# A two-layer transformer with expert routing on one core: GpSimd's scatters and gathers without their waits for TensorE's signals, and ten scatters, not sixteen, in the attention block

## The chip, the core and the metric

The kernel runs on 1 core of one Trainium2 chip. Its engines are TensorE (PE in the profile, PEld for its weight loads), VectorE (DVE), ScalarE (ACT), GpSimd (POOL) and SyncE (SP), which issues transfers. The metric is the device time of one execution in microseconds; a version's time is the median of its runs.

## What is computed

Two layers over 1024 tokens of 256 features, each with attention and a mixture of experts, and a layer norm ahead of each of the four parts:

```
x = x + L0_attn(layernorm(x))      # 16 heads, softmax attention over a triangular solve
x = x + L0_ffn(layernorm(x))       # 64 experts of width 96, top 8, at most 256 tokens each
x = x + L1_attn(layernorm(x))      # linear attention: elu features, cumulative sums
x = x + L1_ffn(layernorm(x))       # 8 experts of width 512, top 2
```

What the change touches is the routing of `L0_ffn`. Each token's normed row goes to its eight experts, and the eight results come back weighted:

```
xbuf = zeros((E, C, D)).at[e_sorted, pos].set(x[tok_sorted], mode='drop')
y = einsum('ecf,edf->ecd', silu(g) * u, w_down)     # g, u: projections of xbuf
out = zeros((N, D)).at[tok_sorted].add(y[e_sorted, safe_pos] * (s_sorted * valid)[:, None])
```

## The kernel before

The kernel has three blocks, one after the other; at the end of a block every engine drains and they meet in a barrier. Their ends are lines L341, L1342 and L1694 in the profile.

**Attention block** (to L341): the first layer's attention. The tokens are in two halves of four tiles of 128 rows (`HT` = 4, `NT` = 8). The first half is done earlier than the second: its rows are normed, its expert choice is made, and GpSimd begins to scatter it into `expert_rows` in DRAM, while the rest of the attention is still being done. `scatter(pool, k, t, rows)` (L199) sends the 128 rows of tile t to the slot of each row's k-th expert. A half has 32 scatters (k = 0 to 7, t = 0 to 3), and the first `EARLY` of the first half stand in this block.

**Expert block** (to L1342): the second half's norm, its choice of experts, the other scatters of the first half (L1527 to L1533), the 32 of the second (L1535 to L1546), and then the 64 experts. A token's eight slots are in the order of their experts, so the k-th slot of a token belongs to expert k or a later one. Therefore SyncE loads the rows of expert e (`load_rows`, L1572) for e below 8 when the scatters of k = e of all eight tiles have landed (`s_gb[e]` at 128). Weights come two experts at a time (`load_weights`); SyncE issues the fourth group behind `load_rows` of expert 7. Per expert TensorE turns the rows (`s_t`), does gate and up (`s_gu`), turns the hidden values (`s_th0`) and projects down (`s_y0`); two experts are in flight. At the end GpSimd gathers the results of k = 0 and 1 (16 gathers, L1558), as soon as the experts that these can name are stored.

**Last block** (to L1694): GpSimd gathers k = 2 to 7 (48 gathers, L2116; gather g uses buffer g % 16 and may start when addition g - 16 is done, `s_acc0`). VectorE adds each gathered tile to `X` (`add_gathered`, L1939). The tokens are in four quarters of twelve gathers (`GQ`), and each quarter goes through the linear attention while the next is added up: norm (`norm_lin`), TensorE turns (`s_tr`) and projects (`s_pr`), ScalarE makes the features (relu and exp, L1874 to L1880), VectorE makes products and running sums (`window`, L1950 to L1957), and TensorE projects out (`s_oo`). VectorE's order is written out:

```
for q in range(1, NQ):
    gathered(q, 0, 3)
    if q > 1:
        add_outputs(q - 2)
        norm_ffn(q - 2)
    add_bias(q - 1)
    gathered(q, 3, 8)
    window(q - 1, 0)
    gathered(q, 8, 11)
    window(q - 1, 1)
    gathered(q, 11, GQ)
    norm_lin(q)
```

Behind it come the second choice of experts, 16 scatters, and 23 tiles of the second mixture of experts.

Many of GpSimd's transfers have a wait for a semaphore that TensorE raises and whose work they don't read: these are the waits of the change. Beside them stand waits that the data need: `s_idx` (slots ready), `s_zf` (rows zeroed), `s_st` (results stored), `s_acc0` (buffer free).

## Time and profile before

| | before |
|---|---|
| median of 3 runs | 1025.71 us (1023.77 to 1027.04) |
| profiled execution, its own time | 1016.34 us |
| its span, first to last instruction | 1014.6 us |
| mean granted TensorE clock | 0.837 of full |
| busy: TensorE / VectorE / ScalarE / GpSimd | 70% / 54% / 31% / 25% |
| indirect transfers by GpSimd | 64 scatters, 16 + 48 gathers, 16 scatters, 23 additions to the output |

All times in rows are microseconds from the start of the span of the one profiled execution, if not marked ns. A busy share is a mean over blocks that have different limits. A name with q (POOLq, DVEq) is the engine's sequencer, which waits, drains and branches; it runs ahead of the engine. GpSimd's busy time for an indirect transfer is the time to issue it, and the transfer lands later. What a row names as the releaser of a wait is inferred.

### The profile page before, as it was taken

Reading aid. Unit: us, or ns where it says so; the run is one execution under the profiler, and the core shown is the slowest. Engines: PE = TensorE matmul, PEld = TensorE weight load, DVE = VectorE, ACT = ScalarE, POOL = GpSimd, SP = SyncE. Lnnn points to the kernel's source line nnn. Section 1 sums busy time; section 2 is a strip of 40 time slices with the busy share of each in tenths; the row PEclk is TensorE's granted clock in tenths of the full one; section 3 lists DMA queues with packets and bytes.
Section 4 is the critical chain, followed back from the end, with each engine's and each line's share of the span. In section 5 each row is a group of like instructions: output and inputs, shape, how many; then the busy total and the mean of one; then the engine's idle time right before and its main releaser. Section 6 shows DMA issues by size and latency. Waiting matters only on the chain. (4 is left out here: it accounts for less than half of the span.)

```text
span 1014.6 us, 17699 instructions
## 1 busy us (share of the span) xinstructions
PE 708.1 (70%) x6542; PEld 566.9 (56%) x6587; DVE 549.2 (54%) x1652; ACT 313.5 (31%) x535; POOL 252.2 (25%) x258
## 2 busy tenths in 40 slices
PE   4858377858757786973156999999205763599995
PEld 2423265446436545842145999999204542599994
DVE  6896986799499679263501333333146675022221
ACT  1004143542444355432022444444003451111110
POOL 6003011120211111016762000000575626023222
PEclk9988779979887898597577999999756675699998
DMA  4981002340631358204947888887422204688760
GB/s 136 137 130 48 0 2 46 156 63 3 199 51 14 125 211 319 96 17 146 320 142 251 288 290 291 294 283 248 130 76 68 81 26 156 244 229 249 221 195 1
DMA packets 75561, 151.73 MB, mean 150 GB/s; under 512 B 12768, under 2 KB 36064, under 8 KB 72544
## 3 DMA queue, kind: packets, MB, share of 16 engines
q1 hardware_dynamic: 62064, 124.27, 39.7%
q0 software_dynamic: 10224, 21.12, 7.4%
q10 hardware_dynamic: 3200, 5.38, 1.6%
q8 instruction: 44, 0.72, 0.3%
q14 instruction: 29, 0.24, 0.1%
HBM read 91.01 MB, written 60.43 MB: 149 GB/s over the span
## 5 line engine op out<-in xcount | busy, mean ns | idle before, releaser
L1375 PE MATMUL scores<-wgu,zero 128*128 128x192 f32 x512 | 98.2, 337 | 3.7 <-DMA wd<-in_wd 3.7
L750 DVE TENSOR_REDUCE block_maxima<-scores 128x10 f32<-128x1280 f32 x64 | 92.3, 1486 | 7.7 <-PE scores L400 6.7
L1032 ACT ACTIVATE E<-scores 128x1280 f32<-128x1280 f32 x64 | 77.3, 1238 | 60.6 <-PE scores L411 32.4
L1476 DVE TENSOR_TENSOR gated_up<-gated,scores 128x192 f32<-128x192 f32 x64 | 22.7, 354 | 123.7 <-ACT gated L1517 123.7
L1375 PEld LDWEIGHTS scores<-wgu,zero 128*128 128x128 f32 x512 | 85.6, 197 | 3.9 <-DMA wd<-in_wd 3.9
L1815 PE MATMUL scores<-xgT,w 128*128 128x128 f32 x736 | 87.8, 278 | 0.0
L1815 PEld LDWEIGHTS scores<-xgT,w 128*128 128x128 f32 x736 | 86.0, 196 | 0.1
L1170 POOL TENSOR_SCALAR_AFFINE_SELECT E<-E 128x256 f32<-128x256 f32 x64 | 27.2, 449 | 205.8 <-ACT E L1032 205.7
L1508 ACT COPY zero<-misc 128x512 f32<-128x512 f32 x64 | 37.5, 586 | 98.3 <-PE misc L1368 98.3
L1392 PE MATMUL scores<-wd,gated_turned 96*128 96x256 f32 x256 | 67.0, 385 | 0.5 <-ACT gated_turned L1504 0.5
L2116 POOL DMA_INDIRECT gb<-expert_outputs,gather_slots x48 | 55.0, 1147 | 33.7 <-DVE X L1939 17.0
L1368 PE MATMUL misc<-cf,xg 128*128 128x128 f32 x256 | 40.3, 281 | 32.7 <-DMA xg<-expert_rows 32.7
L2141 POOL DMA_INDIRECT out<-yb,add_to x23 | 35.5, 1544 | 111.0 <-DVE yb L2079 109.0
L1558 POOL DMA_INDIRECT gb<-expert_outputs,gather_slots x16 | 16.4, 1024 | 171.5 <-DMA expert_outputs<-xnT 164.9
L1468 DVE COPY xnT<-scores 128x512 f32<-128x512 f32 x64 | 44.3, 692 | 25.6 <-PE scores L1392 25.6
L2092 DVE TENSOR_TENSOR cum<-low,scores 128x512 f32<-128x512 f32 x23 | 15.8, 689 | 77.2 <-issue 67.8
L1368 PEld LDWEIGHTS misc<-cf,xg 128*128 128x128 f32 x256 | 32.4, 144 | 41.5 <-issue 19.5
L400 PE MATMUL scores<-cb 128*128 128x128 bf16 x256 | 53.5, 230 | 1.8 <-issue 0.7
L825 DVE TENSOR_TENSOR tmp<-Y,LB 128x120 f32<-128x120 f32 (+35 forms) x244 | 49.7, 242 | 0.3
L834 DVE TENSOR_TENSOR Y<-Y,tmp 128x120 f32<-128x120 f32 (+35 forms) x244 | 49.6, 242 | 0.1
L199 POOL DMA_INDIRECT expert_rows<-stack_q,scatter_slots x32 | 31.5, 984 | 66.4 <-issue 61.3
L1392 PEld LDWEIGHTS scores<-wd,gated_turned 96*128 96x128 f32 x256 | 44.5, 194 | 4.4 <-ACT gated_turned L1504 0.7
(295 smaller groups left out, 1500.4 us busy)
## 6 DMA issues: line engine op xcount, KB each, us to landing
w<-in_w SPq DMA_DIRECT2D x23, 1024.0 KB, 5.0
expert_rows<-zero SPq DMA_DIRECT2D x32, 512.0 KB, 6.2
xg<-expert_rows SPq DMA_DIRECT2D x64, 256.0 KB, 3.2
expert_outputs<-xnT SPq DMA_DIRECT2D x64, 256.0 KB, 3.0
wgu<-in_wgu SPq DMA_DIRECT2D x32, 384.0 KB, 3.6
rows_by_expert<-zero SPq DMA_DIRECT2D x21, 408.0 KB, 6.0
wd<-in_wd SPq DMA_DIRECT2D x32, 192.0 KB, 3.8
w<-in_w ACTq DMA_DIRECT2D x8, 512.0 KB, 10.3
```

What stands on the lines that cost most here:

```text
L400: ins = nc.tensor.matmul(scores[:, slot, o + w - P:o + w], identb, mask[c, it], start=False, stop=True)
L750: nc.vector.tensor_reduce(bm[:, c, h, :], scores[:, slot, 0:WIDE].rearrange("p (a n) -> p a n", n=P), AX.X, ALU.max).then_inc(s_fd, 1)
L825: nc.vector.tensor_tensor(part, Yc[:, x, 0:n, k:k + 1].to_broadcast([P, n, w]), LB[:, k:k + 1, k + 1:SB].to_broadcast([P, n, w]), ALU.mult ...
L834: nc.vector.tensor_tensor(below, below, part, ALU.add).then_inc(s_inv, 1)
L1032: nc.scalar.activation(to[:, h, :], scores[:, k % 2, 0:WIDE], ACT.Exp, scale=SCALE).then_inc(s_fa, 1)
L1368: ins = nc.tensor.transpose(misc[:, j % 2, c:c + P], xg[:, j, t, k * P:(k + 1) * P], identf)
L1375: ins = nc.tensor.matmul(scores[:, j % 2, t * 2 * F0:(t + 1) * 2 * F0], xgT[:, j % 2, k, t * P:(t + 1) * P], wgu[:, j // GE, j % GE, k, :] ...
L1392: ins = nc.tensor.matmul(scores[:, j % 2, 1024 + t * D:1024 + (t + 1) * D], hT[:, j % 2, t * P:(t + 1) * P], wd[:, j // GE, j % GE, :], st ...
L1468: nc.vector.tensor_copy(yb[:, j % NY].rearrange("p t d -> p (t d)"), scores[:, j % 2, 1024:1536]).then_inc(s_yv, 1)
L1508: nc.scalar.copy(xgT[:, j % 2].rearrange("p k n -> p (k n)"), misc[:, j % 2, :]).then_inc(s_xt0, 1)
L1815: ins = nc.tensor.matmul(scores[:, j, c:c + P], w13[:, q, k, c:c + P], xgT[:, j, k, :], start=(k == 0), stop=(k == KT - 1))
L2116: pool.indirect_dma_start(out=gb[:, g % NG, :], out_offset=None, in_=ybuf, in_offset=bass.IndirectOffsetOnAxis(ap=ig[:, t, k:k + 1], axis= ...
```

## The change

The waits for `s_us`, `s_o`, `s_ot`, `s_tr`, `s_lg`, `s_rk`, `s_y0`, `s_t`, `s_th0`, `s_gu`, `s_oo` and `s_pr` ahead of GpSimd's scatters and gathers are taken out, and `EARLY` is 10 in place of 16. No other engine's program changes.

```diff
-EARLY = 16
+EARLY = 10
...
                     for g in range(EARLY):
-                        if g == 4:
-                            pool.wait_ge(s_us, 4 * UNITS)
-                        if g == 6:
-                            pool.wait_ge(s_o, 2 * UNITS - 1)
-                        if g == 8:
-                            pool.wait_ge(s_o, 2 * UNITS)
-                        if g == 9:
-                            pool.wait_ge(s_ot, 2 * UNITS)
-                        if g == 11:
-                            pool.wait_ge(s_tr, 10)
                         scatter(pool, g // HT, g % HT, xn0[:, g % HT, :])
...
                     for g in range(EARLY, HT * K0):
-                        if g == EARLY + 4:
-                            pool.wait_ge(s_tr, 12)
-                        if g == EARLY + 8:
-                            pool.wait_ge(s_lg, 2)
-                        if g == EARLY + 12:
-                            pool.wait_ge(s_rk, 2)
                         scatter(pool, g // HT, g % HT, xn0[:, g % HT, :])
                     pool.wait_ge(s_idx, 4)
                     for k in range(K0):
                         for t in range(HT):
-                            if t == 0 and k > 5:
-                                pool.wait_ge(s_y0, k - 5)
-                            if t == 1 and k > 1:
-                                pool.wait_ge(s_t, k - 1)
-                            if t == 2 and k > 4:
-                                pool.wait_ge(s_th0, k - 4)
-                            if t == 3 and k > 2:
-                                pool.wait_ge(s_gu, k - 2)
                             scatter(pool, k, HT + t, xn[:, t, :])
...
                         if g == NT:
                             pool.wait_ge(s_st[1], 16 * ((E0 - K0) // NY + 1))
-                        if g % 2:
-                            pool.wait_ge(s_gu, min(E0, E0 - 2 + g // 2))
-                        elif g:
-                            pool.wait_ge(s_y0, min(E0, E0 - 5 + g // 2))
...
                     for g in range(NG, NT * K0):
                         t, k = gather_at(g)
-                        q, r = divmod(g - NG, GQ)
                         pool.wait_ge(s_acc0, g - NG + 1)
-                        if r == 3 and q > 1:
-                            pool.wait_ge(s_oo, QT * (q - 1))
-                        if r == 4 and q:
-                            pool.wait_ge(s_tr, 12 + at_lin(q - 1) + 1)
-                        if r == 7 and q:
-                            pool.wait_ge(s_pr, 2 * q - 1)
-                        if r == 8 and q > 1:
-                            pool.wait_ge(s_tr, 12 + at_ffn(q - 2) + 1)
-                        if r == 10 and q:
-                            pool.wait_ge(s_pr, 2 * q)
```

GpSimd's program at the end of the attention block, as a difference (each row is one or more scatters; in brackets the semaphores waited for, by their names, `attended` being `s_o` and `transposed` being `s_tr`):

```order
-L199 DMA expert_rows<-stack_q,scatter_slots 16384x256 x3
-L199 DMA expert_rows<-stack_q,scatter_slots 16384x256 [waits solve_u]
-L199 DMA expert_rows<-stack_q,scatter_slots 16384x256
-L199 DMA expert_rows<-stack_q,scatter_slots 16384x256 [waits attended]
-L199 DMA expert_rows<-stack_q,scatter_slots 16384x256
-L199 DMA expert_rows<-stack_q,scatter_slots 16384x256 [waits attended]
-L199 DMA expert_rows<-stack_q,scatter_slots 16384x256 [waits o_turned]
-L199 DMA expert_rows<-stack_q,scatter_slots 16384x256
-L199 DMA expert_rows<-stack_q,scatter_slots 16384x256 [waits transposed]
-L199 DMA expert_rows<-stack_q,scatter_slots 16384x256 x4
+L199 DMA expert_rows<-stack_q,scatter_slots 16384x256 x9
 L341 UNCONDITIONAL_BRANCH
```

Ahead of these rows stands one more scatter in both. Six scatters have moved behind the block's end.

GpSimd's program at the start of the expert block, before, from the block's first scatter (`stack_q` holds the first half's rows, `xn_moe` the second's):

```order
L199 DMA expert_rows<-stack_q,scatter_slots 16384x256 x4
L199 DMA expert_rows<-stack_q,scatter_slots 16384x256 [waits transposed]
L199 DMA expert_rows<-stack_q,scatter_slots 16384x256 x3
L199 DMA expert_rows<-stack_q,scatter_slots 16384x256 [waits logits]
L199 DMA expert_rows<-stack_q,scatter_slots 16384x256 x3
L199 DMA expert_rows<-stack_q,scatter_slots 16384x256 [waits ranks]
L199 DMA expert_rows<-stack_q,scatter_slots 16384x256 x3
L199 DMA expert_rows<-xn_moe,scatter_slots 16384x256 [waits slots_ready]
L199 DMA expert_rows<-xn_moe,scatter_slots 16384x256 x8
L199 DMA expert_rows<-xn_moe,scatter_slots 16384x256 [waits rows_turned]
```

and the same stretch of the changed kernel, up to the gathers at the block's end:

```order
L1515 UNCONDITIONAL_BRANCH [waits barrier_Pool_Activation_PE_DVE_SP_gather]
L199 DMA expert_rows<-stack_q,scatter_slots 16384x256 x22
L199 DMA expert_rows<-xn_moe,scatter_slots 16384x256 [waits slots_ready]
L199 DMA expert_rows<-xn_moe,scatter_slots 16384x256 x31
L1530 DMA gb<-expert_outputs,gather_slots 128x256 [waits y_stored2,y_stored3,y_stored1,y_stored0]
```

The 16 scatters of the first half that stood here are 22, and the only wait left among the 54 is the one for the slots.

GpSimd's gathers in the last block, before, from the first of quarter 1 that has such a wait (the 16 ahead of it wait for `row_added` alone; `lin_projected` is `s_pr`, `lin_out` is `s_oo`):

```order
L2116 DMA gb<-expert_outputs,gather_slots 128x256 [waits transposed,row_added]
L2116 DMA gb<-expert_outputs,gather_slots 128x256 [waits row_added] x2
L2116 DMA gb<-expert_outputs,gather_slots 128x256 [waits lin_projected,row_added]
L2116 DMA gb<-expert_outputs,gather_slots 128x256 [waits row_added] x2
L2116 DMA gb<-expert_outputs,gather_slots 128x256 [waits lin_projected,row_added]
L2116 DMA gb<-expert_outputs,gather_slots 128x256 [waits row_added] x4
L2116 DMA gb<-expert_outputs,gather_slots 128x256 [waits lin_out,row_added]
```

In the changed kernel all 48 are one row that waits for `row_added`.

## Rows read from the trace of the kernel before

**Rows 1.** Windows: length, busy us (instructions) by engine, granted clock, DMA share, GB/s.
```profile
600.00:700.00 100.00, 100.00 (x639) 93.27 (x638) 36.83 (x71) 41.60 (x106) 0.00 (x0) 1.00 0.85 291
```

**Rows 2.** Timeline of GpSimd's scatters: start, length; in brackets idle time before, releaser.
```profile
451.40 1.18 POOL L199 DMA_INDIRECT expert_rows<-stack_q,scatter_slots  x1 [52.88 <-issue]
...
470.78 0.97 POOL L199 DMA_INDIRECT expert_rows<-stack_q,scatter_slots  x1 [0.31 <-issue]
474.86 0.97 POOL L199 DMA_INDIRECT expert_rows<-stack_q,scatter_slots  x1 [3.12 <-POOLq L341]
...
481.02 0.97 POOL L199 DMA_INDIRECT expert_rows<-stack_q,scatter_slots  x1 [1.34 <-PE misc L163]
...
512.19 0.97 POOL L199 DMA_INDIRECT expert_rows<-xn_moe,scatter_slots  x1 [4.30 <-issue]
...
540.29 0.97 POOL L199 DMA_INDIRECT expert_rows<-xn_moe,scatter_slots  x1 [0.30 <-issue]
```

**Rows 3.** Timeline of TensorE in the first experts.
```profile
510.00 1.09 PE L1368 MATMUL misc<-cf,xg 128*128 128x128 f32 x4 [19.37 <-DMA xg<-expert_rows]
...
549.75 2.61 PE L1375 MATMUL scores<-wgu,zero 128*128 128x192 f32 x7 [3.66 <-DMA wd<-in_wd]
```

**Rows 4.** The block ends' lines: drains, ns min/median/max, first and last start.
```profile
L341 POOLq DRAIN  x1: 11013/11013/11013, 462.9 to 462.9; - x1
L341 DVEq DRAIN  x1: 17/17/17, 465.4 to 465.4; - x1
...
L1342 POOLq DRAIN  x1: 13496/13496/13496, 720.9 to 720.9; - x1
```

**Rows 5.** Timeline of GpSimd's gathers at the expert block's end.
```profile
709.42 1.03 POOL L1558 DMA_INDIRECT gb<-expert_outputs,gather_slots  x1 [2.24 <-PE scores L1375]
...
728.12 1.02 POOL L1558 DMA_INDIRECT gb<-expert_outputs,gather_slots  x1 [0.30 <-issue]
```

**Rows 6.** GpSimd's waits from 760 to 820: total, times, longest.
```profile
POOL gb L2116 <- DVE X L1939: 9.6, 6, 3.8
...
POOL gb L2116 <- PE misc L1730: 2.9, 1, 2.9
```

**Rows 7.** Timeline of GpSimd's gathers in the last block.
```profile
737.86 4.84 POOL L2116 DMA_INDIRECT gb<-expert_outputs,gather_slots  x1 [0.30 <-DVE X L1939]
743.01 1.02 POOL L2116 DMA_INDIRECT gb<-expert_outputs,gather_slots  x1 [0.30 <-issue]
...
784.27 1.02 POOL L2116 DMA_INDIRECT gb<-expert_outputs,gather_slots  x1 [3.00 <-DVE X L1939]
```

**Rows 8.** Line 2107, GpSimd's wait for `s_oo`: ns min/median/max, first and last start.
```profile
L2107 POOLq EVENT_SEMAPHORE  x2: 17/17/17, 783.5 to 804.3; - x2
```

**Rows 9.** Timeline of VectorE: both windows of quarters 0, 1 and 2 begin.
```profile
773.32 0.68 DVE L1950 TENSOR_TENSOR relu<-relu,low 128x512 f32<-128x512 f32 x1
...
775.62 0.87 DVE L1939 SCALAR_TENSOR_TENSOR X<-gb,w,X 128x256 f32<-128x256 f32 x2
...
777.19 0.68 DVE L1950 TENSOR_TENSOR relu<-relu,low 128x512 f32<-128x512 f32 x1
...
794.01 0.69 DVE L1950 TENSOR_TENSOR relu<-relu,low 128x512 f32<-128x512 f32 x1
...
797.92 0.68 DVE L1950 TENSOR_TENSOR relu<-relu,low 128x512 f32<-128x512 f32 x1
...
814.60 0.68 DVE L1950 TENSOR_TENSOR relu<-relu,low 128x512 f32<-128x512 f32 x1
...
818.60 0.69 DVE L1950 TENSOR_TENSOR relu<-relu,low 128x512 f32<-128x512 f32 x1
```

**Rows 10.** Timeline of ScalarE: the last relu of the first window's features, quarters 0 to 2.
```profile
770.58 0.82 ACT L1880 ACTIVATE relu<-scores,bias_lin 128x256 f32<-128x256 f32 x2
...
792.74 0.82 ACT L1880 ACTIVATE relu<-scores,bias_lin 128x256 f32<-128x256 f32 x2
...
813.38 0.82 ACT L1880 ACTIVATE relu<-scores,bias_lin 128x256 f32<-128x256 f32 x2
```

## The prediction

> **What bounds the kernel now.** I read the windows view first, to see which engine has no idle time in which stretch, then GpSimd's own timeline, and then, for each of its pauses, what stands behind it. In the middle of the expert stage TensorE is busy 100.00 of 100.00 us at full granted clock [rows 1], so nothing that GpSimd does there counts. Before it, however, GpSimd is the pacer: from 451.40 to 541.27 us it issues 64 scatters, each 0.97 us long and 1.28 us after the last one [rows 2] (from 512.19 to 540.29 there are 22 steps, 28.10 us, 1.277 us each). SyncE may load expert e's rows only when all eight scatters of k = e have landed, and it issues the fourth weight group behind the load for k = 7. TensorE starts its full run at 549.75 after a wait for exactly that group's `wd` [rows 3]. So whatever ends the last scatter earlier starts the full TensorE run earlier.
>
> The chain of scatters has three pauses beside its usual gap of 0.30 us [rows 2]: 3.12 us at 474.86 (the end of the block), 1.34 us at 481.02 (a released wait for TensorE's transposes) and 4.30 us at 512.19. The last one is put down to "issue", but it stands before the tenth scatter of the second half, which is t = 1, k = 2, and waits for `s_t` at 1. TensorE's first turned rows start at 510.00 and take 1.09 us [rows 3]: the release at 511.09 lies 1.1 us before the scatter.
>
> **The block ends.** GpSimd is last there, too. In the attention block its 16th scatter ends at 471.75, its drain at 462.9 + 11.01 = 473.9, and VectorE had reached its own drain at 465.4 [rows 4]. In the expert block the 16th gather ends at 729.14 [rows 5] and the drain at 720.9 + 13.50 = 734.4 [rows 4]. The drain outlives the last transfer's issue by 2.14 us there and by 5.3 us here. With 16 indirect transfers since the last drain at the first, 64 at the second, the tail grows by about 3.14 / 48 = 0.065 us for each, if it is their number that counts; that it is the number is my reading of two points.
>
> **The change, term by term.** The sum is made against the profiled execution (1016.34 us, span 1014.6). The three runs lie at 1023.77 to 1027.04, 9.4 us above it at the median. I carry the difference over to the median, since nothing shown tells where those 9.4 us lie.
>
> 1. EARLY from 16 to 10. Six scatters leave the attention block: its tenth ends at 471.75 - 6 x 1.28 = 464.1 and its drain, with a tail of 2.14 (or 1.75 by the count), at 466.2 (465.8). Both are later than VectorE's 465.4, so GpSimd still ends the block, 7.7 us earlier. It restarts 0.97 us behind its drain as before (473.9, 474.86), at 467.2. The six scatters are not saved, they come behind the restart: 22 of them, 28.1 us. The second half then starts at 467.2 + 28.1 = 495.3, plus 0.1 for a few that last longer. Before, it started at 540.29 - 31 x 1.277 - 4.0 (the pause of term 2) = 496.7. So 1.3 us are won, the removed wait at 481.02 (1.34 - 0.30 = 1.04) among them. The slots of the second half come from VectorE; it starts this block 7.7 us earlier, so they come no later than the scatters want them.
> 2. The waits on `s_t`, `s_gu`, `s_th0`, `s_y0` between the second half's scatters. Only the pause at 512.19 has a price: 4.30 - 0.30 = 4.0 us. The others stood at 0.30 us and cost nothing. GpSimd's last scatter ends 5.3 us earlier, and with it come the load for k = 7, the weights behind it and TensorE's full run: **-5.3 us**.
> 3. The waits between the 16 gathers at the end of the expert block. The second gather waited 2.24 us for TensorE [rows 5], 1.9 above the usual gap. These gathers end the block, so all of it counts: **-1.9 us**. The drain's tail has six scatters more behind it, +0.4 us by the count and nothing otherwise; the first block's tail is shorter by the same. I take 0 for the two together.
> 4. The waits between the 48 gathers of the last block. GpSimd is idle there 9.6 us in six pauses put down to VectorE's additions, and 2.9 us in one put down to TensorE [rows 6]. The name in the first is misleading: the gather at 784.27 [rows 7] is number 43 and needs only the 28 additions ahead of `norm_lin(0)`, a quarter and more back; the sequencer's own wait on `s_oo` (L2107) stands at 783.5, 0.8 us ahead of it [rows 8]. These pauses go too. But the gathers run 16 buffers ahead and VectorE has a second supplier, the projections by TensorE and ScalarE that feed `window`. What is won is only the time from "features ready" to "window started". VectorE starts the first window of quarters 0 to 2 at 773.32, 794.01 and 814.60 [rows 9]; ScalarE's last `relu` ends at 771.40, 793.56 and 814.20 [rows 10]. With some 0.05 us of signalling that is 1.87, 0.40 and 0.35 us. Between the two windows stand three additions at 0.40 us, and the first window takes 2.30 us (773.32 to 775.62), so 3.50 us from window to window where there were 3.87, 3.91 and 4.00 [rows 9]: 0.37, 0.41 and 0.50 us. Sum: **-3.9 us**. Everything behind `norm_lin(3)` is ordered by VectorE, TensorE and the slots, with no removed wait in it.
>
> The moved instructions cost nothing else: no transfer is added, SyncE's and ScalarE's queues keep their order, and only start 7.7 us sooner. Sum: 5.3 + 1.9 + 3.9 = 11.1 us. 1016.34 - 11.1 = 1005.2 for a profiled execution, 1025.71 - 11.1 = **1014.6 us** for the median.
>
> **Bounds.** If the last block took over all of GpSimd's 12.5 us in those seven pauses less seven usual gaps (2.1), it would win 10.4 in place of 3.9, in all 17.6: 1008.1. If it won nothing, 7.2 in all: 1018.5. For the drains, an end below: both tails at the shorter 2.14 would give 3.2 more.
>
> **Rivals.**
> - *Only the expert stage pays.* The quarters stay as long as they are, because some step of TensorE's and ScalarE's chain that I read as ready is held by another. Rows 9 and 10 speak against it, since each window starts 0.4 us or more behind the `relu` that it reads. 1018.5 us. Chance 17%.
> - *The pauses are the profile's.* The runs are 9.4 us longer than the profiled execution, so their waits may fall otherwise, and TensorE may be late by more or GpSimd by less. Then the gain is lost in what TensorE does: within 3 us of 1025.7. Chance 9%.
> - *The freed gathers hold up VectorE* (slower). While VectorE did 16 additions in a row, a gather lasted 4.84 us in place of 1.02 [rows 7]: the two share something. So far it is the gather that pays. Released from their waits, gathers start whenever they can, also ahead of VectorE's own instructions. In quarters 1 to 3 VectorE has some 30 instructions on the chain with two SBUF operands (18 in the windows, 12 additions). If each waited for half a gather, 0.51 us, that is 15.3 us, and the kernel ends 4.2 us slower, at 1029.9. It decides from 11.1 / 30 = 0.37 us each. Against it: gathers already run beside the windows, and from 772 to 820 VectorE's additions there last the same 0.4 to 0.5 us as without them. Chance 7%, with all other losses. By the Trainium skill, page "SBUF — State Buffer", section "Who interferes with whom", a VectorE instruction with two SBUF inputs contends with a GpSimd instruction that reads SBUF, and issue order decides who blocks. By that rule this rival is the outcome when gathers come first; the trace agrees with it only for gathers that come second.
> - *More than the sum.* The last block gives back up to 10.4 us, or a denser TensorE keeps a higher granted clock in the quarters. Down to 1008.1 us. Chance 9%.
> - *The forecast*, 58%, with a range of its own of 1011 to 1018.
>
> **The numbers.** A change under 0.3% (3.1 us) can't be told from none. Faster by more: 58 + 17 + 9 = 84%; within: 9%; slower: 7%. The range leaves out the no-gain and slower cases above and a little of the fastest below: 1008 to 1021.5 us, which also takes in the spread of the runs (3.3 us).
>
> **What the changed profile would show.** GpSimd's drain in the attention block ends near 466; its scatters then run from about 467 to 536 with no gap over 0.5 us; TensorE's full run starts at about 544.5. In the gathers at the expert block's end no pause is left, and the expert block's drain ends near 727.2. There, additions r = 3 to 7 of a quarter come in a row, followed by idle time that ends with ScalarE's `relu` and not with a landing. I would be wrong if the scatters get a new pause (for VectorE's slots at 495, say), if the drains grow, or if VectorE's instructions lengthen beside the gathers.

## The result: slower by 2.7%, and the profile after

| | before | after |
|---|---|---|
| median | 1024.91 us (4 runs, 1023.77 to 1027.04) | 1052.61 us (4 runs, 1051.89 to 1053.72) |
| ratio | | 1.0269, 95% interval 1.0248 to 1.0289 |
| profiled execution, its span | 1016.34, 1014.6 us | 1053.72, 1052.0 us |
| mean granted clock | 0.837 | 0.826 |

The forecast was 1014.6 us. The time is 38 us above it and lies outside the range.

GpSimd's own pauses went as forecast. This is its timeline after, every row of the scatters whose gap is not the usual 0.30 or 0.31 us, and the last of the attention block and of all. It answers to [rows 2].

```profile
453.20 1.17 POOL L199 DMA_INDIRECT expert_rows<-stack_q,scatter_slots  x1 [52.43 <-issue]
...
464.90 0.97 POOL L199 DMA_INDIRECT expert_rows<-stack_q,scatter_slots  x1 [0.31 <-issue]
480.53 0.97 POOL L199 DMA_INDIRECT expert_rows<-stack_q,scatter_slots  x1 [14.66 <-POOLq L341]
...
516.70 0.97 POOL L199 DMA_INDIRECT expert_rows<-xn_moe,scatter_slots  x1 [8.42 <-DVE gather_slots L1442]
...
556.23 0.97 POOL L199 DMA_INDIRECT expert_rows<-xn_moe,scatter_slots  x1 [0.30 <-issue]
```

Behind the first step of 1.48 us the ten scatters run 1.28 us apart, and the 32 of the second half take 39.5 us from first to last where they took 43.6. But two new gaps stand between them: 14.66 us at the block's end, 8.42 us for VectorE's slots. The last scatter starts at 556.23, 15.9 us later than before.

GpSimd no longer ends the attention block. Its drain is over at 457.8 + 9.96 = 467.8, VectorE's begins at 479.6. These rows, sequencers' drains at the block end, answer to [rows 4]; the last one is the expert block's, which ends at 754.5.

```profile
L341 POOLq DRAIN  x1: 9956/9956/9956, 457.8 to 457.8; - x1
L341 ACTq DRAIN  x1: 614/614/614, 472.3 to 472.3; - x1
L341 DVEq DRAIN  x1: 17/17/17, 479.6 to 479.6; - x1
```
```profile
L1332 POOLq DRAIN  x1: 18762/18762/18762, 735.7 to 735.7; - x1
```

Why VectorE is 14 us later shows in ScalarE's timeline of that stretch. It copies two results of TensorE (L551) into the tiles `bankT` and `bankD`, called the two banks here. Before:

```profile
454.71 0.59 ACT L1074 COPY bankT<-misc 128x512 f32<-128x512 f32 x1 [6.42 <-PE misc L551]
456.92 0.59 ACT L1074 COPY bankD<-misc 128x512 f32<-128x512 f32 x1 [1.63 <-PE misc L551]
```

After, ScalarE and then VectorE:

```profile
460.41 0.58 ACT L1074 COPY bankT<-misc 128x512 f32<-128x512 f32 x1 [10.34 <-remote]
467.68 0.59 ACT L1074 COPY bankD<-misc 128x512 f32<-128x512 f32 x1 [6.68 <-remote]
```
```profile
467.74 0.26 DVE L893 RECIPROCAL rec<-scores 128x16 f32<-128x16 f32 x1 [11.51 <-remote]
```

```
matmul ends   semaphore changes   late by   semaphore
454.81        460.39               5.58     s_o, first bank
461.02        467.66               6.64     s_o, second bank
462.52        467.71               5.20     s_ot
497.91        511.78              13.87     s_rk
793.93        803.76               9.83     s_pr
810.66        819.22               8.57     s_oo
```

By the profile TensorE's matmul is done (its end is a modelled time), the semaphore that says so changes 5 to 14 us later in these six cases, and whoever reads it sits idle. The view of waits puts 129.7 us to "remote" in 17 waits of the changed kernel, and none in the first profile of before. All 17 are waits for a semaphore that TensorE raises. Not every signal is late: of the 89 that fall while GpSimd issues scatters or gathers one behind the other, 37 have no recorded change within 0.25 us of their matmul's end, and of the other 616 one. The longest groups of "remote" (total, times, longest):

```profile
ACT gated L1507 <- remote: 22.3, 2, 18.4
DVE slot L1431 <- remote: 15.6, 1, 15.6
ACT xnT L1834 <- remote: 12.5, 1, 12.5
DVE rec L893 <- remote: 11.5, 1, 11.5
ACT bankT L1074 <- remote: 10.3, 1, 10.3
ACT low L1846 <- remote: 9.9, 1, 9.9
```

The late signals are not all of the 14.2 us. The second bank is copied 10.8 us later (467.68 for 456.92): 6.6 us of it is the late signal, and 4.2 us is that its matmuls themselves end later. These are the 64 matmuls of both banks, before and after:

```profile
450.65 6.20 PE L551 MATMUL misc<-E,xnT 128*32 128x512 f32 x64 [1.07 <-DVE xnT L881]
```
```profile
452.45 6.08 PE L551 MATMUL misc<-E,xnT 128*32 128x512 f32 x57 [1.08 <-DVE xnT L881]
458.96 0.44 PE L551 MATMUL misc<-E,xnT 128*32 128x128 f32 x5 [0.43 <-issue]
460.39 0.63 PE L551 MATMUL misc<-E,xnT 128*32 128x128 f32 x2 [0.99 <-issue]
```

The second bank's 32 took 2.2 us before and 6.2 us after, with gaps for which the profile shows no cause ("issue") and at a granted clock of 1.00 from 453 to 459. The last 3.4 us come behind the copy. While the second bank's last matmuls came with those gaps, TensorE's granted clock fell to its lower level: it was 0.50 (1.2 GHz) from 461 to 477, where it was 1.00 (2.4 GHz) from 456 to 466 before. Its three groups behind the copy took 9.0 us in place of 5.6 (1.11, 1.97 and 5.95 us for 0.66, 1.09 and 3.81).

GpSimd's gathers and the last block's first scatter (to [rows 5] and [rows 7]):

```profile
727.72 1.06 POOL L1530 DMA_INDIRECT gb<-expert_outputs,gather_slots  x1 [170.52 <-DMA expert_outputs<-xnT]
...
747.63 1.02 POOL L1530 DMA_INDIRECT gb<-expert_outputs,gather_slots  x1 [0.30 <-issue]
757.97 1.28 POOL L2077 DMA_INDIRECT gb<-expert_outputs,gather_slots  x1 [9.32 <-DVE X L1911]
759.56 4.84 POOL L2077 DMA_INDIRECT gb<-expert_outputs,gather_slots  x1 [0.30 <-DVE X L1911]
...
874.01 1.07 POOL L2093 DMA_INDIRECT rows_by_expert<-rows_ffn,slots  x1 [39.94 <-DVE slots L1960]
```

The 16 gathers have no pause left and take 19.9 us from first to last, 2.1 less than before (706.12 to 728.12). They start 21.6 us later. The gather of 4.84 us stands where it stood.

The wait of `slot` for the ranks (`s_rk`) is what delayed the second half's slots and left the gap of 8.42 us. In the last block the pauses of [rows 6] are gone, and the windows come later all the same. These are VectorE's two windows of quarter 0 and the first of quarter 1, which answer to the first three in [rows 9] (773.32, 777.19, 794.01), and ScalarE's `low` that the second of them needed:

```profile
794.02 0.69 DVE L1922 TENSOR_TENSOR relu<-relu,low 128x512 f32<-128x512 f32 x1 [2.80 <-ACT relu L1852]
806.11 0.69 DVE L1922 TENSOR_TENSOR relu<-relu,low 128x512 f32<-128x512 f32 x1 [8.51 <-ACT relu L1852]
833.19 0.69 DVE L1922 TENSOR_TENSOR relu<-relu,low 128x512 f32<-128x512 f32 x1 [5.94 <-ACT relu L1852]
```
```profile
803.78 0.84 ACT L1846 ACTIVATE low<-scores,minus_bias 128x256 f32<-128x256 f32 x2 [9.86 <-remote]
```

From the first window to the second it is 12.1 us where it was 3.87, and to the third 39.2 us where it was 20.7. VectorE's own instructions are no longer than they were, 0.69 us for this one.

### The profile page after: what moved, and what is told of

It is laid out like the page before. It is cut to its first block and busy times, and to the rows that moved or that the text cites. A ratio compares the mean times of both kernels' runs of the same rounds, so it can differ in the third digit from the quotient of the medians.

```text
span 1052.0 us, 17685 instructions
## 1 busy us (share of the span) xinstructions
PE 711.8 (68%) x6542; PEld 568.2 (54%) x6587; DVE 548.2 (52%) x1652; ACT 313.0 (30%) x535; POOL 250.7 (24%) x258
## 5 line engine op out<-in xcount | busy, mean ns | idle before, releaser
L1032 ACT ACTIVATE E<-scores 128x1280 f32<-128x1280 f32 x64 | 77.4, 1237 | 60.7 <-PE scores L411 32.4
L1382 PE MATMUL scores<-wd,gated_turned 96*128 96x256 f32 x256 | 69.1, 393 | 10.9 <-ACT gated_turned L1494 6.3
L2102 POOL DMA_INDIRECT out<-yb,add_to x23 | 35.5, 1543 | 111.2 <-DVE yb L2051 88.1
```

The costliest lines, as they stand in the source:

```text
L1032: nc.scalar.activation(to[:, h, :], scores[:, k % 2, 0:WIDE], ACT.Exp, scale=SCALE).then_inc(s_fa, 1)
L1382: ins = nc.tensor.matmul(scores[:, j % 2, 1024 + t * D:1024 + (t + 1) * D], hT[:, j % 2, t * P:(t + 1) * P], wd[:, j // GE, j % GE, :], st ...
```

## The experiments

All kernels are set against runs of the kernel before on the same chip. That matters: the experiments fell on five chips, and on one of them, here called the fifth, the kernel before took 1014.5 us where it took 1024 to 1027 on the other four. On which chips the result and the first profile of before were taken is not known. The table shows the landmarks of each profile from GpSimd's timeline: the second half's first scatter (h2), the last scatter (end), the first of the 16 gathers (g0), the first of the 48 (g16), the first scatter of the last block (r0), and the span. "Late" is how many of 705 TensorE signals have no recorded change within 0.25 us of their matmul's end. Some records of changes are missing, so this counts too many; the idle time put to "remote" is the safer column.

| kernel | its time | before beside it | late | "remote" us | h2 | end | g0 | g16 | r0 | span |
|---|---|---|---|---|---|---|---|---|---|---|
| before, first profile | 1016.34 | | 0 | 0 | 496.7 | 540.3 | 706.1 | 736.3 | 840.3 | 1014.6 |
| before, profiled again | 1025.4 | 1026.2 | 27 | 48.9 | 502.6 | 547.8 | 713.1 | 744.1 | 845.0 | 1023.7 |
| EARLY 10 alone | 1031.3 | 1024.8 | 31 | 53.9 | 507.7 | 552.8 | 717.6 | 748.1 | 851.3 | 1029.6 |
| attention block's waits out | 1035.7 | 1024.8 | 31 | 37.8 | 511.0 | 556.5 | 720.6 | 751.6 | 855.7 | 1034.0 |
| expert block's waits out | 1031.6 | 1024.8 | 28 | 66.0 | 507.1 | 546.6 | 719.4 | 750.5 | 851.8 | 1030.5 |
| last block's waits out | 1038.8 | 1024.8 | 32 | 81.2 | 501.7 | 547.2 | 713.0 | 743.6 | 859.5 | 1037.4 |
| after | 1052.6 | 1024.9 | 38 | 129.7 | 516.7 | 556.2 | 727.7 | 758.0 | 874.0 | 1052.0 |
| second half's waits out | 1027.0 | 1025.3 | 34 | 60.7 | 501.0 | 540.5 | 713.2 | 743.6 | 847.7 | 1026.1 |
| second half's waits out, on the fifth chip | 1010.5 | 1014.5 | 0 | 0 | 496.8 | 536.4 | 702.9 | 733.4 | 834.2 | 1008.7 |
| end gathers' waits out, on the fifth chip | 1014.0 | 1014.5 | 0 | 0 | 498.6 | 542.5 | 708.0 | 736.1 | 838.5 | 1012.7 |

Theory 1 was that TensorE's signals are handed on late while GpSimd issues indirect transfers without standing still for them. Theory 2 was that what is late is only a consequence: of six more scatters behind the block's end, or of VectorE's instructions held up by GpSimd's.

### The change in four parts

**EARLY 10 alone.** `-EARLY = 16`, `+EARLY = 10`, all waits kept (that at g = 11 goes with its scatter).

> The change split: here only EARLY goes from 16 to 10, and all waits for TensorE stay where they were (the one at g = 11 falls away with its scatter; those counted from EARLY move to scatters 14, 18 and 22). Theory 1 (TensorE's signals are handed on late while GpSimd issues indirect transfers one behind the other with no wait for TensorE between them) gives no loss here: no ScalarE or VectorE wait at 455 to 468, the second block starts 5 to 8 us earlier than before's 474.1 and the whole is 0 to 3 us faster than before, about 1024. Theory 2 (six more scatters behind the block's end are what pushes the experts back) gives the last scatter at 545 or later and a kernel of 1030 or more.

1031.31 us, ratio 1.0066 (1.0035 to 1.0098): slower by itself. Theory 1's numbers were wrong, and theory 2's were met (last scatter at 552.8, over 1030 us): six more scatters behind the block's end do cost time. They do because the block's end does not come sooner by as much, and its rows show why. GpSimd is through early, but VectorE reaches its drain only at 475.3 and not at 465.4 [rows 4], since its inputs are late in this profile too:

```profile
466.52 1.00 POOL L199 DMA_INDIRECT expert_rows<-stack_q,scatter_slots  x1 [0.82 <-PE scores L561]
476.24 0.97 POOL L199 DMA_INDIRECT expert_rows<-stack_q,scatter_slots  x1 [8.72 <-POOLq L341]
```
```profile
L341 POOLq DRAIN  x1: 3128/3128/3128, 466.3 to 466.3; - x1
L341 DVEq DRAIN  x1: 17/17/17, 475.3 to 475.3; - x1
```

The block ends at 475.4 where it ends at 478.1 in the second profile of before, and GpSimd starts again at 476.24 and not at 478.89: 2.6 us won for six scatters (7.7 us) that come behind it. The difference of 5.1 us is that of h2 (507.7 to 502.6).

**The attention block's waits alone.** The five `wait_ge` on `s_us`, `s_o`, `s_ot` and `s_tr` ahead of these scatters are out, EARLY is 16.

> Only the five waits for TensorE in the attention block are taken out, EARLY stays 16. Theory 1: the 16 scatters run from about 451 to 472, and what TensorE signals from 454 on reaches ScalarE and VectorE late; with six scatters more than in the changed kernel the delay is at least its 5.7 us at the block's start, so the second block starts at 480 to 487 and the kernel takes 1031 to 1038. Theory 2 (transfers and instructions only share memory, signals are not held): GpSimd had been paused nowhere in this block, so nothing changes, 1025 within 2 us. The rival of the prediction (GpSimd's instructions make VectorE's longer): VectorE's instructions beside the scatters are longer than before, with no idle time ahead of them.

1035.73 us, 1.0102 (1.0068 to 1.0136), as theory 1 had it. With 16 scatters in a row the second bank's signal comes later still than in the changed kernel, and the block ends at 486.4:

```profile
458.78 0.59 ACT L1074 COPY bankT<-misc 128x512 f32<-128x512 f32 x1 [8.18 <-remote]
473.02 0.59 ACT L1074 COPY bankD<-misc 128x512 f32<-128x512 f32 x1 [13.66 <-remote]
```

**The expert block's scatter waits alone.** All of them on `s_tr`, `s_lg`, `s_rk`, `s_y0`, `s_t`, `s_th0`, `s_gu` ahead of its scatters are out.

> Only the waits for TensorE ahead of the scatters of the expert block are taken out, 16 and 32 of them. Theory 1: VectorE waits for the ranks (8 to 14 us late in the changed kernel), the slots of the second half come late, the last scatter is some 10 us behind before's 540.3, and the kernel takes 1032 to 1038. Theory 2, and term 2 of the prediction by itself: the pause at 512 goes and nothing else moves, last scatter at 535, 1020 to 1022.

1031.55 us, 1.0058 (1.0040 to 1.0076), just under the range of theory 1 and far above theory 2's. The last scatter was not 10 us late. The second half starts 4.5 us later (a wait of 8.6 us for the ranks) but then needs 39.5 us and not 45.2, so it ends 1.2 us sooner. The loss is TensorE's: it stands still in the middle of its first experts, because ScalarE waited 15.5 us ahead of `gated`, put to "remote": TensorE's signal for it came at 552.24, 12.5 us behind the matmul's end.

```profile
507.06 0.97 POOL L199 DMA_INDIRECT expert_rows<-xn_moe,scatter_slots  x1 [7.67 <-DVE gather_slots L1452]
```
```profile
553.03 0.66 PE L1383 MATMUL scores<-cf,gated_up 128*96 128x128 f32 x2 [13.26 <-DVE gated_up L1476]
```

From there to the first gather it is 166.4 us, and 156.1 in the second profile of before (557.0 to 713.1): its full run starts with 10 us more of work still to do.

**The last block's waits alone.** The five `wait_ge` behind `s_acc0` are out.

> Only the waits for TensorE ahead of the 48 gathers of the last block are taken out. Theory 1: between the last block's start and the first of its 16 scatters the changed kernel lost 12 us, so 1034 to 1040 here, with ScalarE and VectorE waiting behind matmuls that had ended 7 to 10 us before. Theory 2 (the loss there is only the consequence of what was late in the earlier blocks) and term 3 and 4 of the prediction: 1021 to 1025. The prediction's rival (VectorE held up by gathers) gives about 1029 with VectorE busy longer in its own instructions and no new idle time.

1038.79 us, 1.0134 (1.0109 to 1.0159). Up to g16 it is as the second profile of before; from g16 to r0 it takes 115.9 us where that took 100.9 (the first profile 104.0) and the changed kernel 116.0. ScalarE's two longest waits there:

```profile
787.31 0.84 ACT L1874 ACTIVATE low<-scores,minus_bias 128x256 f32<-128x256 f32 x2 [8.18 <-remote]
...
808.42 0.58 ACT L1862 COPY xnT<-misc 128x512 f32<-128x512 f32 x1 [14.58 <-remote]
```

VectorE's additions answer the rival of the prediction. By line and shape in this block, of before and of this kernel:

```profile
L1939 DVE SCALAR_TENSOR_TENSOR X<-gb,w,X 128x256 f32<-128x256 f32 x62 | 27.8, 480 | 28.0 <-DMA gb<-expert_outputs,gather_slots 25.8 <-issue 2.1
```
```profile
L1939 DVE SCALAR_TENSOR_TENSOR X<-gb,w,X 128x256 f32<-128x256 f32 x63 | 27.4, 480 | 14.6 <-DMA gb<-expert_outputs,gather_slots 14.5
```

480 ns in both, so freed gathers do not lengthen them, and the idle time that landings put ahead of them is less.

### The kernel before, once more

> The kernel before, unchanged, profiled once more. The first profile showed 1016.3 us where the runs lie at 1023 to 1028, and three kernels that share its attention block word for word (only the last block or the expert block differs, or six scatters at the end) all showed a scatter there held 2.4 us behind a TensorE signal that had ended earlier, with ScalarE 9 us idle ahead of it, which the first profile did not. If late signals belong to the kernel before too, this profile takes 1023 to 1028 and shows the same 2.4 us pause at 464 and some of the others. If they come only from the edits, it shows none and takes about 1016.

1025.4 us. The program is the same as that of the front's rows, the profile is not: 48.9 us of waits for late signals, and 9.1 us more of span. GpSimd's pauses at the same places as [rows 2]:

```profile
465.12 0.97 POOL L199 DMA_INDIRECT expert_rows<-stack_q,scatter_slots  x1 [2.36 <-remote]
...
478.89 0.97 POOL L199 DMA_INDIRECT expert_rows<-stack_q,scatter_slots  x1 [3.11 <-POOLq L341]
...
497.35 0.97 POOL L199 DMA_INDIRECT expert_rows<-stack_q,scatter_slots  x1 [2.39 <-remote]
516.91 0.97 POOL L199 DMA_INDIRECT expert_rows<-xn_moe,scatter_slots  x1 [3.05 <-issue]
```

The waits also show here what they are worth. At 465.12 and 497.35 GpSimd itself waits for the late signal and issues nothing, and the semaphore changes 2.55 and 2.58 us after its last scatter began. VectorE gets the ranks 1.9 us late. In the changed kernel the scatters go on, and the ranks are 13.9 us late. For the banks the difference is small: their signals and that for `s_ot` are 4.2, 5.5 and 4.0 us late here, and 5.6, 6.6 and 5.2 in the changed kernel. A pause of GpSimd is not the only thing that ends the delay, either: the first bank's signal came at 458.44 here and at 460.39 there, in the midst of scatters 1.28 us apart, and the changed kernel's ranks came 4.47 us after its last scatter had begun.

### What it is in GpSimd's work

**A wait that is always met**, `pool.wait_ge(s_tr, 4)`, ahead of every scatter and gather of the changed kernel.

> The changed kernel with a wait that is always met already (for TensorE's transposes at 4) ahead of every scatter and gather. It tells whether any wait instruction is enough. If the mere presence of a wait ahead of a transfer lets the signals through, the time falls back towards 1025. Theory 1 in its narrow form (GpSimd must really stand still until TensorE has signalled) and in its wide form (something must keep GpSimd's sequencer from running ahead) both give no change against the changed kernel: 1050 to 1056.

1052.17 us (2 runs; the changed kernel took 1047.9 to 1053.3 in its four groups of runs). A wait that is always met brings nothing back.

**Waits for its own landings** in the changed kernel, of which these are two places; its other scatters and gathers have such waits too:

```diff
                     for g in range(EARLY, HT * K0):
+                        if g % HT == 2:
+                            pool.wait_ge(s_gb[g // HT - 1], 16 * HT)
...
                     for g in range(NG, NT * K0):
                         pool.wait_ge(s_acc0, g - NG + 1)
+                        b = g - 3
+                        pool.wait_ge(s_gb[b % NG], 16 * (b // NG + 1 + levels(b % NG)))
```

> The changed kernel, where GpSimd is held back by its own transfers and by no signal of TensorE: the third scatter of each group of four waits until the group before has landed, and each gather until the gather three back has landed. Narrow form of theory 1 (only a wait for TensorE's own signal helps): 1050 or more, plus what the new waits cost, up to 10 us. Wide form (any real wait that keeps GpSimd from running ahead helps): less than 1045, and the wait of VectorE for the ranks that was 15.6 us in the changed kernel is under 5 us. If the transfers themselves are what delays the signals (their number, not how they are spaced), 1050 or more as well, with the same waits.

1057.60 us, 1.0314 (1.0266 to 1.0362). The time is as the narrow form had it, the profile lies between the two forms. The ranks were 0.6 us late and no wait of VectorE for them is put to "remote", as the wide form had it. But in the attention block, where the new wait was met before it was reached, the second bank came late as ever, and so did `xnT` in the last block (21.1 us in two waits):

```profile
456.74 0.97 POOL L199 DMA_INDIRECT expert_rows<-stack_q,scatter_slots  x1 [0.31 <-DMA expert_rows<-stack_q,scatter_slots]
```
```profile
464.62 0.59 ACT L1074 COPY bankD<-misc 128x512 f32<-128x512 f32 x1 [8.85 <-remote]
```

Its pauses of 4.2, 4.3 and 3.2 us for landings cost time of their own (h2 at 517.5). That would fit pauses which let a signal through whatever GpSimd waits for, if they fall at the right moment. But it is one signal of one profile, and the nearest pause (1.19 us) ended at 492.69, 0.75 us before the ranks' matmul did, so this is not shown. The time by itself is also what the third form expected, that the number of transfers delays the signals and not their spacing.

**EARLY 0**, so that no scatter stands in the attention block:

> The kernel before with EARLY at 0: no scatter in the attention block, all 64 in the expert block, the other waits for TensorE kept. Theory 1: no TensorE signal is late in the attention block, so ScalarE's two copies of banks there start within 0.1 us of their matmuls, and the second block starts at 464 to 467. Its 32 first scatters then need 41 us, the last of all 64 starts at 548 to 560 and TensorE's full run begins some 15 us later than before: 1032 to 1042. If the held signals in the attention block have another cause than the scatters, ScalarE waits there all the same.

1034.84 us, 1.0100 (1.0069 to 1.0131). ScalarE's copies there come straight behind TensorE, VectorE's drain starts at 467.6, and the late signals begin with the scatters of the next block.

**Memsets, or plain transfers, in the scatters' place**, on top of EARLY 0. The first runs of both fell on the chip without late signals (1024.54 and 1022.43 us, none late), where they could tell nothing. What they were expected to show, and then the same kernels on a chip with late signals:

> EARLY at 0, and in the place of the attention block's scatters 128 small memsets by GpSimd, about 0.1 us each, one behind the other without a wait: GpSimd works and moves no rows. If it is the transfers that hold up TensorE's signals, ScalarE copies its banks without a wait for a late signal, as with EARLY at 0 alone, and VectorE reaches the block's end at 464 to 468. If GpSimd's being busy is enough, ScalarE waits there 5 us or more.

> EARLY at 0, and in the place of the scatters 16 plain transfers on GpSimd's queue, of the same 128 rows each, to a part of the results' buffer that nobody reads before it is overwritten; GpSimd waits once for all of them at the end. If any transfer that GpSimd issues holds the signals up, ScalarE waits for its bank copies 5 us or more, as in the kernel without the attention block's waits. If only indirect ones do, there is no such wait and VectorE reaches the block's end at 464 to 468.

> EARLY at 0 and 16 plain transfers by GpSimd in the place of the attention block's scatters. On a chip with late signals: if plain transfers delay them too, ScalarE waits 5 us or more for its bank copies and VectorE reaches the block's end behind 470; if not, at 464 to 468. On a chip without them it tells nothing new: about 1022.

> EARLY at 0 and 128 memsets of 0.1 us by GpSimd in the place of the attention block's scatters. On a chip with late signals: no late signal while the memsets run if transfers are what it takes, and VectorE at the block's end at 464 to 468; 5 us or more of waiting by ScalarE if a busy GpSimd is enough. On a chip without them: about 1024.

1036.08 us with plain transfers, 1034.62 with memsets, one run each. The 16 plain transfers run from 452.1 to 460.8, over just the moments at which both banks are handed on, and land in 2.1 to 2.7 us each. ScalarE waits for nothing late:

```profile
L1195 POOL DMA_DIRECT2D expert_outputs<-stack_q x16: 539/539/759, 452.1 to 460.3; - x16
```
```profile
454.07 0.58 ACT L1075 COPY bankT<-misc 128x512 f32<-128x512 f32 x1 [4.79 <-PE misc L552]
456.22 0.58 ACT L1075 COPY bankD<-misc 128x512 f32<-128x512 f32 x1 [1.57 <-PE misc L552]
```

The same kernel shows 30 late signals as soon as its scatters begin at 465.78. The memsets ended at 454.4, before the second bank, so they cover the first alone; it was on time. Of what was tried only indirect transfers do it; plain ones on the same queue, with the same rows and as many semaphore steps, did not, in one profile.

### Two parts of the change on a chip without late signals

**The second half's waits alone**, term 2 of the prediction, and **the end gathers' waits alone**, term 3:

> Term 2 of the prediction by itself: of before's waits only those for s_t, s_gu, s_th0 and s_y0 ahead of the second half's 32 scatters are taken out. The prediction: pauses gone, 4 to 5 us faster, 1020 to 1021. Theory 1: the scatters do end some 5 us earlier (from first to last of the second half 40 us, 45 in the second profile of before), but TensorE's first experts are held meanwhile, with the 10 us of arrears that the kernel without any such wait in this block showed, so the 64 experts end no earlier and the kernel takes 1024 to 1030.

> Term 3 by itself: only the waits between the 16 gathers at the expert block's end are taken out. From the first of these gathers to the first of the last block took 31.0 us in the second profile of before and 30.3 in the changed kernel: theory 1 has the pauses that go balanced by TensorE's last signals coming later, and gives 1023 to 1027. Term 3 gives 1.9 us less, which is at the edge of what can be told.

Before took 1014.54 us here (19 runs). Without the second half's waits it is 1010.49 us, 0.9957 (0.9941 to 0.9973), 4.05 us faster. The 32 scatters have no pause, 39.6 us from first to last in place of 43.6, and TensorE's full run starts at 546.25, 3.5 us before [rows 3]:

```profile
546.25 2.93 PE L1375 MATMUL scores<-wgu,zero 128*128 128x192 f32 x8 [4.00 <-DMA wd<-in_wd]
```

Without the end gathers' waits it is 1014.01 us, 0.9991 (0.9975 to 1.0007). The gathers run 1.32 us apart throughout and g0 to g16 takes 28.1 us, 2.1 less than in the first profile; in the time this can't be told from nothing.

On a chip with late signals the first of the two gains nothing:

> The kernel before without the second half's waits for s_t, s_gu, s_th0 and s_y0. Where before takes 1014: 4 us faster, as measured. Where before takes 1025: TensorE's first experts are held behind late signals and the 4 to 5 us are given back, 1024 to 1030.

1027.01 us beside 1025.34, 1.0009 (0.9991 to 1.0026). The last scatter starts 7.3 us sooner than in the second profile of before, and the first gather at 713.2 as there (713.1). TensorE lost the time again in waits: ScalarE stood 12.5 us before one gate and 10.2 before one `zero`, both "remote".

### The changed kernel on other chips

> The changed kernel, unchanged. If before, beside it, takes about 1014 (a chip without late signals): the prediction's terms give 11.1 us less than before, 1003, and at least the 4 us that the second half's scatters alone gave, so under 1010; theory 1 in its plain form (GpSimd's unpaced transfers always delay TensorE's signals) gives late signals and 1040 or more even there. If before takes about 1025: 1052 again, with late signals.

> The changed kernel, unchanged, on whichever chip. Where before takes about 1014 beside it: the prediction's terms give 1003 and the second half's scatters alone 1010; theory 1 in its plain form, late signals and over 1040. Where before takes about 1025: 1052 to 1054 as twice before, with 30 to 40 late signals.

> The changed kernel, unchanged, once more. Where before takes about 1014 beside it: 1003 by the prediction's terms, under 1010 in any case; theory 1 in its plain form, over 1040. Where before takes about 1025: 1047 to 1054 with 30 to 40 late signals, as on the chips so far.

These were three more chances to meet a chip without late signals, and none was one. Before took 1025.34, 1026.91 and 1023.96 us beside it, the changed kernel 1053.33 (1.0290, 1.0268 to 1.0311), 1047.87 (1.0193, 1.0123 to 1.0262) and 1051.42 us (1.0272, 1.0245 to 1.0300), with 115.1, 100.5 and 111.2 us of "remote" waits. What it does on a chip without late signals was not measured.

## Why the prediction was wrong

**The step that failed** is in the sum: "The moved instructions cost nothing else", with the cost of the removed waits at nothing wherever the gap stood at 0.30 us and "some 0.05 us of signalling" behind each matmul. It took TensorE's signals to arrive when its work is done, whatever GpSimd does. On the chips where the time was taken many don't. While GpSimd issues indirect transfers one behind the other, 37 of 89 were late in the changed kernel, the six listed above by 5 to 14 us, and the readers' waits for late ones summed to 129.7 us where the kernel before has 48.9. The removed waits had kept GpSimd from going on at those moments: taken out in one block alone they cost 10.9, 6.7 or 14.0 us. The profile that I read held no late signal, 0 in 705.

**The sign that I passed over.** "I carry the difference over to the median, since nothing shown tells where those 9.4 us lie." As far as the second profile tells, they lay in late signals. The second profile of before has 9.1 us more span: 5.9 by h2, 1.6 more by the last scatter, and what came between there and the end summed to 1.6. A profile 9.4 us under the median, where the runs spread over 3.3 us, was of an execution of another kind, perhaps on another chip; the rival "The pauses are the profile's" was drawn from this but had only a range within 3 us of before and 9%. It should have asked what the runs have that the profile has not, and what the change does to that.

**Term 1** (EARLY, -1.3 us): GpSimd's side was right (drain at 467.8 for a forecast 466.2). That VectorE would be at its drain by 465.4 was read from a block without late signals. Where they are late it comes at 475.3 with the waits and at 479.6 without, GpSimd waits for it, and the six scatters moved cost 5.1 us of h2. The constant alone made the kernel 6.5 us slower.

**Term 2** (-5.3 us, the last scatter): without late signals 4.05 us by the runs and 4.0 by the scatters, of which my estimate had 4.0 for the pause; right there. With late signals the same edit gave 0, since TensorE's first experts fall behind by as much. The sentence "whatever ends the last scatter earlier starts the full TensorE run earlier" held (547.3 for 557.0), but the run then starts with more work left, and the first gather does not move.

**Term 3** (-1.9 us): 2.1 us in the profile without late signals, under what the runs can tell (0.5). In the changed kernel the pause went as well, but g0 to g16 took 30.3 us, as in the first profile (30.2): TensorE, VectorE and SyncE reached their drains at 751.0, 753.2 and 756.1, so that SyncE ended the block and not GpSimd, which was through at 754.5.

**Term 4** (-3.9 us): the quarters lost 15.0 us beside the second profile of before (g16 to r0), 12.0 beside the first. The pauses of [rows 6] that TensorE's signals made did go, and then `s_pr`, `s_tr` and `s_oo` came up to 10.1 us late (812.65 to 822.78), where none of the three was late in the second profile of before.

**The sign that came in.** Of the signs of being wrong that the prediction named, the first is there: a new pause of the scatters for VectorE's slots (8.42 us ahead of 516.70). VectorE's instructions did not lengthen, and the drains hardly grew: they ended 1.9 and 5.8 us behind the last transfer's issue, where it was 2.14 and 5.3, and by the count of transfers would have been 1.75 and 5.7.

**The rivals.** "The freed gathers hold up VectorE" had the right sign, the wrong mechanism and a price of 4.2 us: VectorE's additions take 480 ns before and after. The Trainium skill (page "SBUF — State Buffer", section "Who interferes with whom") says that a VectorE instruction with two SBUF inputs contends with a GpSimd instruction that reads SBUF, and that issue order decides which of them blocks. No run here shows VectorE's blocked, with 480 ns for an addition beside paced gathers and beside freed ones. What came late was not an instruction but a signal. Slower had 7%, and not one mechanism of mine lay above 1030.

**The parts and the whole.** Alone they cost 6.5 (EARLY), 10.9 (attention), 6.7 (expert) and 14.0 us (last block), 38.1 together, and the change cost 27.7. They overlap in the attention block. With ten scatters and no waits the second bank comes at 467.7, with sixteen at 473.0, so EARLY 10 costs by itself and may save beside the removed waits; the change with EARLY at 16 was not run. The end gathers' waits are in none of the four; they were taken out alone on the fifth chip only.

**What stays open.** What in an indirect transfer holds TensorE's signals back, and whether the same thing slowed the second bank's matmuls; what ends the delay, since a pause of GpSimd was there in some cases and not in others; why this is so on four chips and not on the fifth (the first profile of before, with no late signal and 1016.3 us, is like those of the fifth, and the timed runs listed with it like those of the four), and whether it is the chip at all: the fifth was used in one session only, so something else of that session could be the cause; and what the changed kernel does on such a chip. The prediction's terms would give 1003 us there, and of them only 2 and 3 were run. No version was faster than the kernel before on the chips with late signals. On the one without, the second half's waits taken out are worth 4 us.

## What to carry to other kernels

A wait that guards no data can still do work: before taking it out, ask what others receive during the pause. When a profiled execution lies outside the spread of the timed runs, profile the same kernel once more before reading any gap of 0.3 us as a cost of zero. An instruction that starts with "remote" behind a matmul that ended long before points at a late signal, and then the engine to look at is neither of the two that stand in the row.

## What the runs showed of the hardware

- While GpSimd issued scatters or gathers 1.28 to 1.32 us apart, 37 of TensorE's 89 semaphore signals were late in the changed kernel, one by 13.9 us, and 27 of 106 in the second profile of before; outside those stretches 1 of 616 and none of 599 were. Where GpSimd paused for the signal itself, it came 2.55 and 2.58 us after its last scatter began (two cases in the second profile of before); another came 4.47 us after it, and some came with no pause at all.
- Indirect transfers do this. Sixteen plain transfers 0.54 us apart on the same queue delayed neither bank's signal, though both fell among them (one profile).
- It was so on four chips (before at 1024 to 1027 us) and not on a fifth (1014.5 us, four profiles, no late signal), with three of the changed programs profiled on both kinds.
- With TensorE held back and idle in the changed kernel its granted clock was 0.50 from 461 to 477. 28 matmuls in three groups behind 468 took 9.0 us where they took 5.6 at a granted clock of 1.00.
